# Splitting the p v products of an eight-key tile by keys instead of heads, with one VectorE sum, and moving GpSimd's residual add to the end of its slot

## The chip, the cores and the metric

One core of one Trainium2 chip runs the program once. The metric is the device time of that execution in microseconds (us).

## What is computed

The input x has shape 8 x 2048 x 512 (n, b, c). Attention runs over the first axis, so every (b, head) pair has a sequence of only 8 positions. The mask lets positions 0 to 3 see keys 0 to 3, and positions 4 to 7 see all eight.

```python
xn = layernorm(x)                                  # over c, eps 1e-5
q, k, v = split(xn @ Wqkv.T + bqkv)                # 16 heads of 32
scores = mask + 32**-0.5 * einsum('bnd,bmd->bnm', q, k)
attn = softmax(scores)
o = einsum('bnm,bmd->bnd', attn, v)
attn_out = o @ Wproj.T + bproj
lin = fp16(fp8(xn)) @ fp16(fp8(Wffn)).T + bffn     # float32 sums
out = x + attn_out + lin
```

## The kernel before

The 16,384 rows are cut into 128 tiles of 128 rows, so a tile is one position n % 8 for 128 values of b. Eight tiles in a row are a group, and their k and v stay in SBUF for the whole group (`k_all`, `v_all`, two groups deep; v is stored with the key as the innermost of its indices). The first four tiles of a group need 4 keys, the last four need 8.

The order is written out by hand. Each engine runs the same list of slots, and in slot j it does, for each stage, the tile j minus the stage's lag (`L_STATS` 1 to `L_PROJ` 15). Sixteen slots (two groups) are the body of a loop, `run_slots`; the first and the last sixteen stand outside it, and seven passes lie inside. Engines meet through counting semaphores alone (`after(...)`), and each works through its own queue strictly in the written order.

Slots are named here by j modulo 16. What bears on the change, per slot:

- **VectorE** (`slot` under `@block.vector`): layer-norm statistics (L722), the sum over keys of the p v products of tile j - 12 (L731), the aggregate of the statistics (L736), the q k products (L694) and their sum (L698) of tile j - 8, the softmax row sum and reciprocal of tile j - 9 (L745, L748), for an eight-key tile a second L694 and L698, then row maximum and shift (L758, L761). An eight-key tile takes two of the 2048-element products and sums, a four-key tile one. The lags make every slot hold three such units: slots 4 to 7 and 12 to 15 have two q k units and one p v sum, slots 0 to 3 and 8 to 11 have one q k unit and two p v sums.
- **GpSimd** (`slot` under `@block.gpsimd`): the probabilities (L399) and the first p v product of tile j - 11 (L388), the residual add of tile j - 15 (L407), the low half of the attention output of tile j - 13 (L412), the power for the inverse deviation of tile j - 2 (L418), the low half of the normalised x of tile j - 3 (L423), and for an eight-key tile the second p v product (L388 again). Slots 7 to 10 and 15, 0, 1, 2 have two products, the others one.
- **ScalarE**: exponential of tile j - 9 (L473), copies and scales for the layer norm (L482 to L510), high half of o (L491), the scaled copy `projected` (L516), the linear part and the preset of `proj_ps` (L522, L527), and the copies of k and v out of PSUM, tile j - 4 (L534, L543).
- **TensorE**: projection of tile j - 15, the linear product of tile j - 14, k and v of tile j - 4, q of tile j - 5.
- **SyncE's queue** issues, in this order: the load of x (L297), the reload for the residual (L301), the store of tile j - 15 (L306, after `y_ready`, the residual add's semaphore), the transpose of o (L316), that of x8 (L324) and that of x16 (L330).

The p v products go through a ring of four buffers of 2048 float32, `prod_pv`. For an eight-key tile, `head_units` gives two units of 8 heads and all 8 keys; for a four-key tile one unit of 16 heads and 4 keys:

```python
v = v_all[:, (n // N) % 2, h * D:(h + heads) * D, 0:keys].rearrange("p (h d) m -> p h d m", d=D)
p = probs[:, n % 2, h:h + heads, 0:keys].unsqueeze(2).broadcast_to([P, heads, D, keys])
```

## Time and profile before

| | |
|---|---|
| median of 3 runs | 1708.37 us (1707.04 to 1708.56) |
| the profiled execution's own time | 1709.81 us |
| its span, first to last instruction | 1707.7 us |
| mean granted TensorE clock in it | 0.978 |
| busy: TensorE, VectorE, GpSimd, ScalarE | 1517.0, 1518.7, 1373.5, 1025.5 us |

The profile is one execution. "Busy" is the time in which an engine executed something; an idle time is put down to the engine and line whose semaphore ended it, and "issue" is idle time for which the profile shows no such event. The span is the clock for all rows; 2.1 us of the execution lie around it.

### The profile page before, as it was taken

The numbers are of one execution on the slowest core, as the hardware profiler recorded it, in microseconds if no ns is written. First come the engines' busy times: TensorE is split into PE (matmuls) and PEld (weight loads), VectorE is DVE, ScalarE is ACT, GpSimd is POOL, SyncE is SP. The second block draws the span as 40 slices with busy tenths as digits, with TensorE's granted clock in tenths as the row PEclk, the third lists the DMA queues.
The fourth block names the chain that finished last, engine by engine and source line by source line (L and its number), as shares of the span: only waits on it lengthen the run. The fifth ranks groups of instructions, "written<-read, shape, count | busy, mean of one in ns | idle before, by whom it ended". The sixth has DMA issues, their size and how long they took to land.

```text
span 1707.7 us, 24850 instructions
## 1 busy us (share of the span) xinstructions
PE 1517.0 (89%) x6791; PEld 677.6 (40%) x6913; DVE 1518.7 (89%) x1380; ACT 1025.5 (60%) x1946; POOL 1373.5 (80%) x854
## 2 busy tenths in 40 slices
PE   4998898989989998998989899898998989899855
PEld 3443343434434443443434344343443434344312
DVE  6499898989989999999989899898998899999892
ACT  5665666656656666556566666666666666666422
POOL 2368879697896979879697887969788796978877
PEclk8999999999999999999999999999999999999978
DMA  5343534445354354444444444444444444453332
GB/s 188 72 99 90 123 99 109 117 99 130 98 124 105 97 130 98 117 112 111 109 105 113 106 116 105 114 111 101 119 105 119 105 105 116 104 124 85 90 71 77
DMA packets 366532, 184.30 MB, mean 108 GB/s; under 512 B 314160, under 2 KB 314160, under 8 KB 366384
## 3 DMA queue, kind: packets, MB, share of 16 engines
q1 hardware_dynamic: 366384, 182.53, 43.9%
q8 instruction: 68, 1.11, 0.3%
q14 instruction: 80, 0.66, 0.2%
HBM read 73.41 MB, written 33.55 MB: 63 GB/s over the span
## 4 chain that ended last, share of the span: by engine, by line
POOL 35%; issue 30%; DVE 26%; PE 4%; ACT 3%; POOLq 1%; DVEq 1%; DMA 0%; ACTq 0%; SPq 0%
POOL prod_pv L388 22%; DVE prod_qk L694 14%; DVE scores L698 6%; POOL o L412 4%; POOL x L423 4%; POOL xs L407 3%; POOL rstd L418 2%; DVE stats L722 2%; PE k_ps L579 1%; PE v_ps L579 1%; POOL probs L399 1%; DVE q_ps L758 1%; DVE row_sum L745 1%; PE q_ps L579 1%; POOLq L79 1%
## 5 line engine op out<-in xcount | busy, mean ns | idle before, releaser
L388 POOL TENSOR_TENSOR prod_pv<-kv,probs 128x2048 f32<-128x2048 f32 x192 | 813.0, 4234 | 16.2 <-POOL probs L399 11.1
L731 DVE TENSOR_REDUCE o_nat<-prod_pv 128x256 f32<-128x2048 f32 (+1 forms) x192 | 436.1, 2284 | 92.3 <-POOL prod_pv L388 72.5
L698 DVE TENSOR_REDUCE scores<-prod_qk 128x64 f32<-128x2048 f32 x192 | 439.4, 2288 | 7.3
L579 PE MATMUL k_ps<-wqkv_hi,xT 128*128 128x512 f16 x1024 | 334.1, 388 | 118.2 <-DMA xT<-x 118.1
L694 DVE TENSOR_TENSOR prod_qk<-q_ps,kv 128x2048 f32<-128x2048 f32 x192 | 432.0, 2250 | 2.5 <-ACT kv L534 2.5
L407 POOL TENSOR_TENSOR xs<-xs,projected 128x512 f32<-128x512 f32 x128 | 162.4, 1269 | 238.5 <-ACT projected L516 237.9
L579 PE MATMUL proj_ps<-wproj_hi,oT 128*128 128x512 f16 x1032 | 336.4, 388 | 6.3 <-ACT proj_ps L527 6.3
L579 PE MATMUL v_ps<-wqkv_hi,xT 128*128 128x512 f16 x1024 | 326.0, 380 | 0.0
L579 PE MATMUL q_ps<-wqkv_hi,xT 128*128 128x512 f16 x1024 | 325.4, 379 | 0.0
L473 ACT ACTIVATE exps<-shifted,exp_scale 128x64 f32<-128x64 f32 (+1 forms) x128 | 47.8, 373 | 365.8 <-DVE shifted L761 365.6
L579 PEld LDWEIGHTS k_ps<-wqkv_hi,xT 128*128 128x128 f16 x1024 | 101.8, 99 | 272.7 <-issue 144.8
L543 ACT ACTIVATE kv<-v_ps 128x512 f32<-128x512 f32 x128 | 141.3, 1104 | 113.9 <-PE v_ps L579 113.8
L579 PE MATMUL proj_ps<-wproj_lo,oT 128*128 128x512 f16 x516 | 201.1, 390 | 0.0
L579 PE MATMUL k_ps<-wqkv_lo,xT 128*128 128x512 f16 x512 | 198.9, 388 | 0.0
L579 PE MATMUL v_ps<-wqkv_lo,xT 128*128 128x512 f16 x512 | 194.5, 380 | 0.0
L579 PE MATMUL q_ps<-wqkv_lo,xT 128*128 128x512 f16 x512 | 194.0, 379 | 0.0
L423 POOL TENSOR_TENSOR x<-xn,x 128x512 f16<-128x512 f32 x128 | 148.3, 1159 | 17.4 <-ACT x L510 17.4
L534 ACT ACTIVATE kv<-k_ps 128x512 f32<-128x512 f32 x128 | 75.4, 589 | 133.1 <-PE k_ps L579 133.1
L412 POOL TENSOR_TENSOR o<-o_nat,o 128x512 f16<-128x512 f32 x128 | 148.3, 1159 | 5.6 <-ACT o L491 5.6
L579 PEld LDWEIGHTS proj_ps<-wproj_hi,oT 128*128 128x128 f16 x1032 | 102.7, 100 | 125.4 <-issue 9.8
L579 PEld LDWEIGHTS v_ps<-wqkv_hi,xT 128*128 128x128 f16 x1024 | 100.5, 98 | 121.8 <-issue 1.7
L579 PEld LDWEIGHTS q_ps<-wqkv_hi,xT 128*128 128x128 f16 x1024 | 100.2, 98 | 120.8
(115 smaller groups left out, 1727.9 us busy)
## 6 DMA issues: line engine op xcount, KB each, us to landing
xn<-in_L_attn_x SPq DMA_DIRECT2D x128, 256.0 KB, 2.8
xs<-in_L_attn_x SPq DMA_DIRECT2D x128, 256.0 KB, 2.9
out<-xs SPq DMA_DIRECT2D x128, 256.0 KB, 2.0
xT<-x SPq DMA_TRANSPOSE x256, 3.0
kv<-in_L_attn_Wqkv SPq DMA_DIRECT2D x3, 1024.0 KB, 10.6
oT<-o SPq DMA_TRANSPOSE x128, 3.2
kv<-in_L_ffn_weight SPq DMA_DIRECT2D x1, 1024.0 KB, 5.6
kv<-in_L_attn_Wproj SPq DMA_DIRECT2D x1, 1024.0 KB, 14.6
```

What stands on the lines that cost most here:

```text
L388: nc.gpsimd.tensor_tensor(o, v, p, ALU.mult).then_inc(pv_multiplied, 1)
L407: nc.gpsimd.tensor_tensor(xs[:, n % 4, :], xs[:, n % 4, :], projected[:, :], ALU.add).then_inc(y_ready, 1)
L412: nc.gpsimd.tensor_tensor(o16[:, n % 2, C:2 * C], o_nat[:, n % 2, :], o16[:, n % 2, 0:C], ALU.subtract).then_inc(o_lo_ready, 1)
L418: nc.gpsimd.tensor_tensor(rstd[:, n % 2, :], var_eps[:, :], minus_half[:, :], ALU.pow).then_inc(rstd_ready, 1)
L423: nc.gpsimd.tensor_tensor(x16[:, n % 2, C:2 * C], xn[:, n % 4, :], x16[:, n % 2, 0:C], ALU.subtract).then_inc(x_lo_ready, 1)
L473: nc.scalar.activation(exps[:, n % 4, :, 0:keys], shifted[:, :, 0:keys], ACT.Exp, scale=exp_scale[:, 0:1]).then_inc(exps_ready, 1)
L534: nc.scalar.activation(k_all[:, g % 2, n % N, :], k_ps[:, :], ACT.Copy).then_inc(k_kept, 1)
L543: nc.scalar.activation(v_all[:, g % 2, :, n % N], v_ps[:, :], ACT.Copy).then_inc(v_kept, 1)
L579: last = nc.tensor.matmul(acc[:, :], t[:, tc, :], w[:, c, col:col + 512], start=first and k == 0, stop=k == len(parts) - 1, skip_group_che ...
L694: nc.vector.tensor_tensor(prod_qk[:, :].rearrange("p (m c) -> p m c", c=C), qb, k, ALU.mult).then_inc(qk_multiplied, 1)
L698: nc.vector.tensor_reduce(scores[:, :, m0:m0 + 4].rearrange("p h m -> p m h"), prod_qk[:, :].rearrange("p (m h d) -> p m h d", h=H, d=D), ...
L731: nc.vector.tensor_reduce(o_nat[:, n % 2, h * D:(h + heads) * D], prod_pv[:, u % PRODS, :].rearrange("p (c m) -> p c m", m=keys), AX_X, AL ...
```

## The change

Two edits.

1. For an eight-key tile the two p v units are now keys 0 to 3 and keys 4 to 7 of all 16 heads (`key_units`, which the q k products use already); the function `head_units` is gone. Each unit's product has the shape that a four-key tile has: 16 heads, 32 channels, 4 keys. The two halves lie in neighbouring buffers of the ring, and VectorE sums both in one `tensor_reduce` over two axes (buffer and key), which waits for the tile's last product and raises `pv_summed` by two.
2. In GpSimd's slot the residual add stands last, behind the second product.

```diff
-            def products(i, n, unit):
-                u, h, heads = unit
-                keys = keys_of(n)
-                v = v_all[:, (n // N) % 2, h * D:(h + heads) * D, 0:keys].rearrange("p (h d) m -> p h d m", d=D)
-                p = probs[:, n % 2, h:h + heads, 0:keys].unsqueeze(2).broadcast_to([P, heads, D, keys])
-                o = prod_pv[:, u % PRODS, :].rearrange("p (h d m) -> p h d m", d=D, m=keys)
+            def products(i, n, u, m0):
+                v = v_all[:, (n // N) % 2, :, m0:m0 + 4].rearrange("p (h d) m -> p h d m", d=D)
+                p = probs[:, n % 2, :, m0:m0 + 4].unsqueeze(2).broadcast_to([P, H, D, 4])
+                o = prod_pv[:, u % PRODS, :].rearrange("p (h d m) -> p h d m", d=D, m=4)
                 after(pool, probs_ready, tile_count(i, n))
-                after(pool, v_kept, tile_count(i, N * (n // N) + keys - 1))
+                after(pool, v_kept, tile_count(i, N * (n // N) + m0 + 3))
                 after(pool, pv_summed, unit_count(i, u - PRODS))
                 nc.gpsimd.tensor_tensor(o, v, p, ALU.mult).then_inc(pv_multiplied, 1)
...
-                    products(i, n, head_units(n)[0])
-                if live(i, j, L_PROJ):
-                    n = j - L_PROJ
-                    after(pool, proj_scaled, tile_count(i, n))
-                    after(pool, res_loaded[n % 4], 16 * ring_count(i, n, 4))
-                    nc.gpsimd.tensor_tensor(xs[:, n % 4, :], xs[:, n % 4, :], projected[:, :],
-                                            ALU.add).then_inc(y_ready, 1)
+                    products(i, n, *key_units(n)[0])
...
-                    for unit in head_units(n)[1:]:
-                        products(i, n, unit)
+                    for unit in key_units(n)[1:]:
+                        products(i, n, *unit)
+                if live(i, j, L_PROJ):
+                    n = j - L_PROJ
+                    after(pool, proj_scaled, tile_count(i, n))
+                    after(pool, res_loaded[n % 4], 16 * ring_count(i, n, 4))
+                    nc.gpsimd.tensor_tensor(xs[:, n % 4, :], xs[:, n % 4, :], projected[:, :],
+                                            ALU.add).then_inc(y_ready, 1)
...
-                    keys = keys_of(n)
-                    for u, h, heads in head_units(n):
-                        after(dve, pv_multiplied, unit_count(i, u))
-                        after(dve, o_lo_ready, tile_count(i, n - 2))
-                        nc.vector.tensor_reduce(o_nat[:, n % 2, h * D:(h + heads) * D],
-                                                prod_pv[:, u % PRODS, :].rearrange("p (c m) -> p c m", m=keys), AX_X,
-                                                ALU.add).then_inc(pv_summed, 1)
+                    units = len(key_units(n))
+                    place = units_before(n) % PRODS
+                    after(dve, pv_multiplied, unit_count(i, last_unit(n)))
+                    after(dve, o_lo_ready, tile_count(i, n - 2))
+                    nc.vector.tensor_reduce(o_nat[:, n % 2, :],
+                                            prod_pv[:, place:place + units, :].rearrange("p q (c m) -> p c q m", m=4),
+                                            AX_XY, ALU.add).then_inc(pv_summed, units)
```

How the instructions stand. On GpSimd, slot 15 of the first pass, ahead of the jump back to the loop's start: L399 and L388 are the probabilities and a product, L407 the residual add, L412, L418 and L423 the low half of o, the power and the low half of x. Before:

```order
L399 TENSOR_TENSOR probs<-exps,inv_sum 128x128 [waits pv_multiplied,inv_ready]
L388 TENSOR_TENSOR prod_pv<-kv,probs 128x2048 [waits pv_summed,v_kept,probs_ready]
L407 TENSOR_TENSOR xs<-xs,projected 128x512 [waits res_loaded0,proj_scaled]
L412 TENSOR_TENSOR o<-o_nat,o 128x512 [waits o_hi_ready]
L418 TENSOR_TENSOR rstd<-var_eps,minus_half 128x1 [waits xn_ready,var_ready]
L423 TENSOR_TENSOR x<-xn,x 128x512 [waits x_hi_q_ready]
L388 TENSOR_TENSOR prod_pv<-kv,probs 128x2048 [waits pv_summed,v_kept,probs_ready]
L93 UNCONDITIONAL_BRANCH
```

and with the change (the lines of the changed program are numbered anew):

```order
L392 TENSOR_TENSOR probs<-exps,inv_sum 128x128 [waits pv_multiplied,inv_ready]
L381 TENSOR_TENSOR prod_pv<-kv,probs 128x2048 [waits pv_summed,v_kept,probs_ready]
L399 TENSOR_TENSOR o<-o_nat,o 128x512 [waits o_hi_ready]
L405 TENSOR_TENSOR rstd<-var_eps,minus_half 128x1 [waits xn_ready,var_ready]
L410 TENSOR_TENSOR x<-xn,x 128x512 [waits x_hi_q_ready]
L381 TENSOR_TENSOR prod_pv<-kv,probs 128x2048 [waits pv_summed,v_kept,probs_ready]
L420 TENSOR_TENSOR xs<-xs,projected 128x512 [waits res_loaded0,proj_scaled]
L88 UNCONDITIONAL_BRANCH
```

The add has gone from the third place to the last, and the jump now follows it instead of a product.

On VectorE, slot 0 of the loop, where an eight-key tile is summed. Before:

```order
L722 BN_STATS stats<-xn 128x6 [waits mean_var_ready]
L79 REGISTER_ALU
L79 ISA [waits stats_ready,minus_mean_ready]
L79 REGISTER_ALU [waits pv_multiplied]
L731 TENSOR_REDUCE o_nat<-prod_pv 128x256 [waits o_lo_ready]
L79 REGISTER_ALU
L731 TENSOR_REDUCE o_nat<-prod_pv 128x256 [waits o_lo_ready,pv_multiplied]
L736 BN_AGGR mean_var<-stats 128x2
```

and with the change:

```order
L715 BN_STATS stats<-xn 128x6 [waits mean_var_ready]
L74 REGISTER_ALU
L74 ISA [waits stats_ready,minus_mean_ready]
L74 REGISTER_ALU [waits pv_multiplied]
L724 TENSOR_REDUCE o_nat<-prod_pv 128x512 [waits o_lo_ready]
L729 BN_AGGR mean_var<-stats 128x2
```

Two sums, each with its own wait for a product, have become one that waits for both products.

SyncE's queue, one slot of the loop, with the change (the same as before but for the line numbers):

```order
L292 DMA xn<-in_L_attn_x 128x512
L296 ISA [waits y_stored2]
L296 DMA xs<-in_L_attn_x 128x512
L301 ISA [waits y_ready]
L301 DMA out<-xs 128x512
L74 REGISTER_ALU
L311 DMA_TRANSPOSE oT<-o 128x8x128 [waits o_lo_ready,proj_summed]
L319 DMA_TRANSPOSE xT<-x 128x2x128 [waits x_hi_q_ready,lin_summed]
L74 REGISTER_ALU [waits x_lo_ready]
L325 DMA_TRANSPOSE xT<-x 128x8x128 [waits q_summed]
```

Nothing moved here: the store, with its wait for the residual add, still stands ahead of the three transposes.

## Rows read from the trace of the kernel before

**Rows 1.** Windows, one pass: length, busy PE, PEld, DVE, ACT, POOL, clock

```profile
755.70:957.50 201.80, 184.47 (x837) 82.36 (x851) 186.29 (x168) 126.15 (x242) 170.71 (x105) 1.00 0.46 110
```

**Rows 2.** Groups by line, shapes apart, VectorE: passes of the loop, then tail

```profile
L731 DVE TENSOR_REDUCE o_nat<-prod_pv 128x256 f32<-128x2048 f32 x112 | 253.5, 2284 | 66.6 <-POOL prod_pv L388 59.3 <-DVE stats L722 6.0
...
L731 DVE TENSOR_REDUCE o_nat<-prod_pv 128x256 f32<-128x2048 f32 x10 | 22.6, 2281 | 7.6 <-POOL prod_pv L388 7.6
...
L731 DVE TENSOR_REDUCE o_nat<-prod_pv 128x256 f32<-128x2048 f32 x7 | 15.9, 2277 | 15.8 <-POOL o L412 10.1 <-POOL prod_pv L388 5.7
```

**Rows 3.** Timeline of VectorE (start us, duration us, what, idle before it)

```profile
853.31 0.69 DVE L722 BATCH_NORM_STATS2 stats<-xn 128x6 f32<-128x512 f32 x1
854.03 4.48 DVE L731 TENSOR_REDUCE o_nat<-prod_pv 128x256 f32<-128x2048 f32 x2
858.43 0.17 DVE L736 BATCH_NORM_AGGREGATE mean_var<-stats 128x2 f32<-128x6 f32 x1
...
863.88 0.69 DVE L722 BATCH_NORM_STATS2 stats<-xn 128x6 f32<-128x512 f32 x1
...
893.97 2.29 DVE L731 TENSOR_REDUCE o_nat<-prod_pv 128x256 f32<-128x2048 f32 x1 [2.96 <-POOL prod_pv L388]
...
914.55 0.69 DVE L722 BATCH_NORM_STATS2 stats<-xn 128x6 f32<-128x512 f32 x1
...
927.66 0.69 DVE L722 BATCH_NORM_STATS2 stats<-xn 128x6 f32<-128x512 f32 x1
...
957.55 0.69 DVE L722 BATCH_NORM_STATS2 stats<-xn 128x6 f32<-128x512 f32 x1 [3.58 <-issue]
```

**Rows 4.** Timeline of GpSimd: starts of slots 9 and 10, then slot 15 into slot 0

```profile
866.85 0.42 POOL L399 TENSOR_TENSOR probs<-exps,inv_sum 128x128 f32<-128x128 f32 x1
...
880.38 0.42 POOL L399 TENSOR_TENSOR probs<-exps,inv_sum 128x128 f32<-128x128 f32 x1
...
945.52 1.27 POOL L407 TENSOR_TENSOR xs<-xs,projected 128x512 f32<-128x512 f32 x1 [4.21 <-ACT projected L516]
...
948.38 1.16 POOL L423 TENSOR_TENSOR x<-xn,x 128x512 f16<-128x512 f32 x1
949.50 4.53 POOL L388 TENSOR_TENSOR prod_pv<-kv,probs 128x2048 f32<-128x2048 f32 x1
953.99 0.40 POOL L399 TENSOR_TENSOR probs<-exps,inv_sum 128x128 f32<-128x128 f32 x1
```

**Rows 5.** GpSimd's products by tile: duration ns, shortest, median, longest

```profile
L388 POOL TENSOR_TENSOR prod_pv<-kv,probs x192: 3637/4523/4558, 91.5 to 1683.6; 128x2048 f32<-128x2048 f32 x192
```

**Rows 6.** Groups by line, shapes apart, VectorE: row sum with 8 and 4 keys

```profile
L745 DVE TENSOR_REDUCE row_sum<-exps 128x16 f32<-128x128 f32 x64 | 17.6, 276 | 0.0
...
L745 DVE TENSOR_REDUCE row_sum<-exps 128x16 f32<-128x64 f32 x64 | 13.4, 209 | 2.8 <-ACT exps L473 2.8
```

**Rows 7.** Timeline of ScalarE: copy of v in slot 10, start of slot 13

```profile
885.93 1.11 ACT L543 ACTIVATE kv<-v_ps 128x512 f32<-128x512 f32 x1 [1.36 <-PE v_ps L579]
...
914.67 0.40 ACT L473 ACTIVATE exps<-shifted,exp_scale 128x128 f32<-128x128 f32 x1 [1.11 <-DVE shifted L761]
...
917.96 0.61 ACT L510 ACTIVATE x<-xn 128x512 fp8e4<-128x512 f32 x1
918.48 0.66 ACT L516 ACTIVATE projected<-proj_ps,out_scale 128x512 f32<-128x512 f32 x1
```

**Rows 8.** Timeline of TensorE: first product of k in slots 10 and 12

```profile
880.54 0.39 PE L579 MATMUL k_ps<-wqkv_hi,xT 128*128 128x512 f16 x1 [1.94 <-DMA xT<-x]
...
907.06 0.39 PE L579 MATMUL k_ps<-wqkv_hi,xT 128*128 128x512 f16 x1 [1.33 <-DMA xT<-x]
```

**Rows 9.** SyncE: a wait in total, times, longest us; two issues of slot 11

```profile
SPq L306 <- POOL xs L407: 763.0, 128, 10.9
...
902.02 1.17 SPq L324 DMA_TRANSPOSE xT<-x  x1
903.37 1.23 SPq L330 DMA_TRANSPOSE xT<-x  x1
```

4 lines of the change are left out of this document (1 added, 3 removed).

## The prediction

> **What bounds the kernel now.** I read the busy time of one pass of the loop first. Of its 201.8 us VectorE works 186.3, TensorE 184.5 and GpSimd 170.7 [rows 1]. No average names a bound there, so a slot-by-slot reading is needed. The lags of the slots decide the rest.
>
> For VectorE I take a slot from one statistics instruction to the next. Without a stall, a slot with two q k units takes 927.66 - 914.55 = 13.11 us, and one with two p v sums takes 863.88 - 853.31 = 10.57 [rows 3]. GpSimd's slots with two products take 880.38 - 866.85 = 13.53 us without a gap in them [rows 4]. These are slots 7 to 10 and 15 to 2, and three of each four fall on VectorE's short slots. There VectorE stands still until the second product is done, 2.96 us at a time [rows 3]. Grouped by line, the two sums of eight-key tiles waited 59.3 us for products inside the passes, 7.6 us in the slots right behind the passes, and 15.8 us in the tail [rows 2].
>
> So two engines take turns: GpSimd in its heavy slots, VectorE in the rest. GpSimd cannot work ahead for its heavy stretch: in slot 15 it sits idle for 4.21 us because the residual add, third in its slot, needs `projected`, which ScalarE delivers late in its own slot [rows 4]. One more stall is in every pass: 3.58 us ahead of VectorE's first instruction after the jump back, ended by nothing the profile shows [rows 3]. Nothing in the change touches it.
>
> **Part 1, the shape of the products.** GpSimd's 192 products have the same number of elements, yet two durations: 3.64 us at the short end, 4.52 in the middle [rows 5]. The 64 short ones are the four-key tiles' (16 heads, 32 channels, 4 keys), the 128 long ones the eight-key tiles' (8 heads, 8 keys; 4.53 us in slot 15 [rows 4]). The change gives those 128 the short form. The first unit reads by the very pattern of a four-key tile. The second starts at the fifth key, 16 bytes further, which no row shows: its price lies between 3.64 and 4.53 us. I take 3.64, because the form is the same and only the start differs. Then a heavy slot takes 13.53 - 2 x 0.89 = 11.75 us.
>
> The Trainium skill speaks against this: its "GPSIMD Engine Reference", section "Performance versus the Vector engine", gives a two-input elementwise instruction a floor of about 2.5 cycles per element, and 4497 ns for 2048 float32, whatever the pattern. That agrees with the eight-key products and not with the four-key ones, which are 0.86 us shorter; if it held for the new ones, nothing would be gained in this part (rival 2 works that case out from rows).
>
> **Part 2, one sum for two.** Two sums occupy VectorE for 858.43 - 854.03 = 4.40 us, 2.20 each [rows 3]. The row sum costs 276 ns for 128 elements and 209 for 64 [rows 6], so 1.05 ns per element; 2048 of them are 2.14 us and the fixed part is 0.06. One instruction for 4096 elements saves that once: 64 x 0.06 = 3.8 us. It reads 16-byte pieces from two places 8 KB apart in turn. The nearest row, the 64-element row sum, also takes 16-byte pieces (at a step of 32) and pays nothing per element for it. Bounds: 4.33 us as reckoned; an upper one no row gives (rival 3).
>
> The new wait is the larger matter: the sum cannot start on the first half. Queued behind it on VectorE are the aggregate and the next q k product. It must not come before GpSimd's second product is done, which Part 4 checks.
>
> **Part 3, the add at the end.** Let S be the start of VectorE's slot. ScalarE starts at S + 0.12; the low half of x can start when x8 is done, at S + 4.0, and `projected` is done at S + 4.6 [rows 7]. With the add last, GpSimd no longer waits for `projected` ahead of 4.5 us of product, but for x8, ahead of 1.1 + 3.6.
>
> What the add is moved past: the low halves of o and x, the second product, and, through `y_ready`, SyncE's queue. There the store stands ahead of the three transposes, and already waits 763.0 us in total for the add [rows 9]. Call E the end of the add. In a heavy slot E comes one product and one add after the low half of x, and only then the transposes are issued: about 0.5 us for the store (an estimate from its short issue), 1.5 for the transpose of o (estimated by the next one), 903.37 - 902.02 = 1.35 for that of x8, and 3.7 from the last one's issue to TensorE's first k product (903.37 to 907.06 [rows 8, 9]), so **k starts at E + 7.1**. The copy of v follows 885.93 - 880.54 = 5.4 us later and takes 1.1 [rows 7, 8], and ScalarE's next slot starts behind it, at E + 13.6. That is two slots after the one of E.
>
> The jump follows the add (1.27 us) instead of a product (4.53), which hid GpSimd's own refetch, since its next instruction starts without a gap [rows 4]. If it costs what VectorE's does, 3.58 + 0.29 - 1.27 = 2.6 us are uncovered. VectorE stands still there too, so I count nothing.
>
> **Part 4, does GpSimd keep up?** Slot 7: low half of x at S + 4.0 to 5.2, second product to 8.8, E at 10.0. Slot 8 (S is 13.1 later): probabilities and first product end at S + 1.0, the rest waits for x8 again: E = S + 10.0. Slot 9 (10.6 later): first product to S + 3.5, three small steps to 6.3, second product to 9.9, E = 11.1. Slot 10: second product ends at S + 11.0. VectorE wants it for the sum of slot 11 at S(11) + 0.7, which is S(10) + 11.3. So it is in time by 0.3 us, and all earlier ones by more. The way through the transposes: E of slot 8 is S(10) - 11.2, so ScalarE starts slot 10 at S + 2.4 instead of 0.1, x8 is done at 6.3, and the second product ends at 11.1: in time by 0.2. TensorE idles some 2 us in slots 8 and 9, and makes it up in 12 to 15, where its 184.5 / 16 = 11.5 us per slot stand against 13.1.
>
> After the jump VectorE's stall gives 3.5 us more room. **So every slot is VectorE's**, with two places where a few tenths decide.
>
> **The sum.** From 1707.7: products' waits in the passes 59.3, after them 7.6 [rows 2], the merged sums 3.8. The tail is GpSimd's. Its heavy slots lack the power and the low half of x there (1.16 us, and some 0.5 of the 3.98 from the add's start to the second product's [rows 4]), so they take 11.8 us and will take 10.0: three of them give 5.4. The last sum costs 2.1 more, since both halves follow the last product. An estimated 0.5 comes back where a wait for `projected` no longer precedes a product. That is 3.8. Together 74.5, a span of 1633.2, with the 2.1 around it 1635.3. The median stands 1.4 below the profiled execution: **1634 us**.
>
> **Rivals.**
>
> 1. *The queue behind the store costs more.* The slack of 0.2 us is gone if the transposes land, say, 2 us later (three are now issued in one burst), or if only the second product keeps 4.53. Then slots 10 and 11 stall 2 us, twice a pass less what the jump hides, say 20 us in seven passes and 2 behind them: **1656 us**. For it: the small slack, and that all 128 stores come first. Against: even tied to this path throughout, two heavy slots would take 13.6 + 9.8 = 23.4 us against 27.0 now, so it cannot undo the gain.
> 2. *The form brings nothing:* products of 4.53 us from a cause other than the form. Heavy slots stay at 13.5; the second product of slot 8 ends at S + 9.7, that of slot 9 13.5 later, at S(9) + 12.6, where the sum of slot 10 wants it at S(9) + 11.3 (a stall of 1.3), and that of slot 10 another 13.5 later, 2.9 after the sum of slot 11 is due. Behind the jump the same reckoning, with 2.6 us uncovered there, gives 0.7 and 2.9. That is 7.8 a pass against 59.3 / 7 = 8.5 now, and with the merged sums a gain of 10: **1698 us**. Against: the four-key rows have no other difference than form.
> 3. *Slower: the two-axis sum pays for its jumps.* The gain is 74 us over 64 sums, so it decides from 1.2 us more per sum, 5.5 instead of 4.3. At twice the time per element (8.6 us) 64 sums add 64 x 4.3 = 275 us in slots that VectorE bounds: **1909 us**. For it: no row shows such a read. Against: the row sums. The Trainium skill's "SBUF — State Buffer", section "Door 1: The DMA port swizzle", has full bandwidth for accesses that stay in a 16-byte line, which each piece of four float32 does; no run here shows it for this pattern.
>
> **How the numbers follow.** Forecast 0.74, rival 1 0.12, rival 2 0.07, rival 3 0.05, something else near no change 0.02. The range holds the forecast and rival 1. Below it reaches to 1616: the 6.0 us of waits between statistics and sum [rows 2] could go as well, and the 5.7 us of product waits in the tail. Above it reaches to 1684, for a rival 1 of twice the size. A measurement can tell 0.2%, 3.4 us, from no change. Faster: 0.92 (forecast, rivals 1 and 2, less 0.01); same 0.02; slower 0.06.
>
> **What would show it.** Right: all 192 products near 3.64 us; 64 sums near 4.35 us; VectorE's idle time before p v sums in the passes below 10 us; a pass of about 193 us; k starting late after its transpose in slots 8 to 11; GpSimd's waits no longer ahead of the add but ahead of the low halves. Wrong: products of two durations in one tile, sums above 5 us, or VectorE waiting for q, k or the exponential, which would mean that the path through the transposes binds.

## The result, and the profile after

The changed kernel takes **1623.88 us** (median of 4 runs, 1623.51 to 1624.54) where the kernel before takes 1708.46 beside it (4 runs, 1707.04 to 1709.53): a ratio of 0.9506, with an interval of 0.9489 to 0.9522. It is faster by 84.6 us. The forecast was 1634 with a range of 1616 to 1684, so the direction and the range were right, and the point lies 10 us above the time. That small miss is the sum of larger ones with opposite signs, and most of what follows is about them.

The profiled execution took 1623.51 us, its span 1621.7. First the page of the changed kernel: the busy time of each engine, and one of the queues.

```profile
PE 1503.6 (93%) x6791; PEld 677.0 (42%) x6913; DVE 1512.6 (93%) x1316; ACT 1032.9 (64%) x1946; POOL 1265.4 (78%) x854
...
q14 instruction: 50, 0.41, 0.1%
```

GpSimd is busy for 1265.4 us where it was 1373.5. The second line is a queue that fetches instructions, in packets of 8 KB (0.41 MB / 50). There were 80 packets before and there are 50 now, five fewer for each of the loop's six jumps.

The window of the same pass of the loop answers to [rows 1], with the same columns:

```profile
718.95:909.18 190.23, 183.66 (x834) 82.25 (x849) 185.56 (x161) 127.02 (x241) 156.78 (x105) 1.00 0.48 117
```

A pass takes 190.23 us instead of 201.80. VectorE works 185.56 of them, so this pass is VectorE's but for 4.7 us, as Part 4 had it. GpSimd has 33 us to spare.

GpSimd's products, by tile (count; shortest, median, longest in ns), answer to [rows 5]:

```profile
L381 POOL TENSOR_TENSOR prod_pv<-kv,probs x192: 3634/3642/3656, 91.1 to 1592.3; 128x2048 f32<-128x2048 f32 x192
```

All 192 have one duration. VectorE's groups by line with the shapes apart answer to [rows 2]. The first three rows are of the whole span, the fourth of the passes alone, the fifth of the stretch from the last statistics instruction to the end.

```profile
L724 DVE TENSOR_REDUCE o_nat<-prod_pv 128x512 f32<-128x4096 f32 x64 | 282.9, 4420 | 24.7 <-POOL prod_pv L381 16.7 <-DVE stats L715 3.6 <-ACT minus_mean L477 1.8
...
L715 DVE BATCH_NORM_STATS2 stats<-xn 128x6 f32<-128x512 f32 x128 | 88.2, 689 | 14.4 <-DMA xn<-in_L_attn_x 11.9 <-issue 2.2
```
```profile
L724 DVE TENSOR_REDUCE o_nat<-prod_pv 128x512 f32<-128x4096 f32 x56 | 247.5, 4420 | 10.7 <-DVE stats L715 3.4 <-POOL prod_pv L381 3.0 <-ACT minus_mean L477 1.8
...
L724 DVE TENSOR_REDUCE o_nat<-prod_pv 128x512 f32<-128x4096 f32 x8 | 35.4, 4419 | 14.1 <-POOL prod_pv L381 13.7 <-DVE stats L715 0.2 <-issue 0.2
```

In the passes the sums wait 3.0 us for products, where they waited 59.3 [rows 2]. The stall ahead of the first statistics instruction after the jump, 20.5 us over six jumps before (of which [rows 3] show one of 3.58), is down to 2.2. Nothing in the forecast had that.

VectorE's timeline in the slots that answer to [rows 3]: the sum of slot 8, that of slot 11, which still waits, and the jump.

```profile
814.98 4.42 DVE L724 TENSOR_REDUCE o_nat<-prod_pv 128x512 f32<-128x4096 f32 x1
...
845.68 0.69 DVE L715 BATCH_NORM_STATS2 stats<-xn 128x6 f32<-128x512 f32 x1
846.73 4.42 DVE L724 TENSOR_REDUCE o_nat<-prod_pv 128x512 f32<-128x4096 f32 x1 [0.37 <-POOL prod_pv L381]
...
909.18 0.69 DVE L715 BATCH_NORM_STATS2 stats<-xn 128x6 f32<-128x512 f32 x1 [0.31 <-issue]
```

The sum of slot 11 waits 0.37 us, once a pass. The forecast had it in time by 0.3 (by 0.2 on the other way). GpSimd's timeline answers to [rows 4]: slot 15 before, a heavy slot, then the jump.

```profile
802.92 1.16 POOL L399 TENSOR_TENSOR o<-o_nat,o 128x512 f16<-128x512 f32 x1 [4.25 <-ACT o L484]
...
805.18 1.16 POOL L410 TENSOR_TENSOR x<-xn,x 128x512 f16<-128x512 f32 x1 [0.59 <-ACT x L503]
...
824.24 0.41 POOL L392 TENSOR_TENSOR probs<-exps,inv_sum 128x128 f32<-128x128 f32 x1
...
835.98 0.41 POOL L392 TENSOR_TENSOR probs<-exps,inv_sum 128x128 f32<-128x128 f32 x1
...
904.48 1.27 POOL L420 TENSOR_TENSOR xs<-xs,projected 128x512 f32<-128x512 f32 x1
905.71 0.41 POOL L392 TENSOR_TENSOR probs<-exps,inv_sum 128x128 f32<-128x128 f32 x1
```

A heavy slot takes 835.98 - 824.24 = 11.74 us (13.53 before; 11.75 forecast). GpSimd's idle time now stands ahead of the low halves. Across the jump it has no gap, though only the short add precedes it: the 2.6 us of a possible gap, which the forecast took to be covered by VectorE's stall, do not occur at all. The waits over the span say the same (us, times, longest):

```profile
POOL o L399 <- ACT o L484: 199.0, 79, 5.8
...
POOL x L410 <- ACT x L503: 60.3, 83, 1.8
PE k_ps L572 <- DMA xT<-x: 47.6, 38, 6.8
...
POOL xs L420 <- ACT projected L509: 24.2, 42, 4.1
```

The wait for `projected` was 237.9 us and is 24.2. TensorE's for the transposes of x is less than half of the 118.1 it was.

**Where 86.0 us of the span went.** The first stretch ends at the first statistics instruction of the loop, the second at the last one of all (1559.50 before, 1479.52 after), the third at the tail's first heavy sum (1656.10 and 1570.28), the fourth at the end.

| stretch | before | after | gained | forecast |
|---|---|---|---|---|
| before the loop | 148.2 | 147.9 | 0.3 | 0 |
| passes | 1411.3 | 1331.6 | 79.7 | 59.3 + 3.4 = 62.7 |
| slots behind them | 96.6 | 90.8 | 5.8 | 7.6 + 0.2 = 7.8 |
| tail | 51.6 | 51.4 | 0.2 | 3.8 + 0.2 = 4.0 |

In the passes 56 us are the idle time ahead of the sums (66.6 to 10.7), 18.3 the stall at the jump, 3.4 the merged sums, and 2 are spread.

### The profile page after: what moved, and what is told of

Its sections match the earlier page's. It is cut to its first block, busy times and chain, and to the rows that moved or that the text cites. A ratio compares the mean times of both kernels' runs of the same rounds, so it can differ in the third digit from the quotient of the medians.

```text
span 1621.7 us, 24736 instructions
## 1 busy us (share of the span) xinstructions
PE 1503.6 (93%) x6791; PEld 677.0 (42%) x6913; DVE 1512.6 (93%) x1316; ACT 1032.9 (64%) x1946; POOL 1265.4 (78%) x854
## 4 chain that ended last, share of the span: by engine, by line
POOL 43%; issue 29%; DVE 10%; PE 7%; ACT 1%; POOLq 1%; DMA 0%; SPq 0%; DVEq 0%; ACTq 0%
POOL prod_pv L381 28%; DVE prod_qk L687 5%; POOL xs L420 5%; POOL x L410 4%; POOL o L399 3%; DVE scores L691 2%; POOL rstd L405 2%; POOL probs L392 2%; PE k_ps L572 2%; PE v_ps L572 2%; PE proj_ps L572 1%; PE q_ps L572 1%; DVE stats L715 1%; POOLq L74 1%; PE lin_ps L610 0%
## 5 line engine op out<-in xcount | busy, mean ns | idle before, releaser
L381 POOL TENSOR_TENSOR prod_pv<-kv,probs 128x2048 f32<-128x2048 f32 x192 | 699.4, 3642 | 16.2 <-POOL probs L392 11.1
L724 DVE TENSOR_REDUCE o_nat<-prod_pv 128x512 f32<-128x2048 f32 (+1 forms) x128 | 429.1, 3353 | 27.0 <-POOL prod_pv L381 16.7
L572 PE MATMUL k_ps<-wqkv_hi,xT 128*128 128x512 f16 x1024 | 328.0, 381 | 49.4 <-DMA xT<-x 47.6
L399 POOL TENSOR_TENSOR o<-o_nat,o 128x512 f16<-128x512 f32 x128 | 148.6, 1161 | 199.0 <-ACT o L484 199.0
L420 POOL TENSOR_TENSOR xs<-xs,projected 128x512 f32<-128x512 f32 x128 | 162.5, 1270 | 24.7 <-ACT projected L509 24.2
L509 ACT ACTIVATE projected<-proj_ps,out_scale 128x512 f32<-128x512 f32 x128 | 87.4, 683 | 86.0 <-PE proj_ps L572 74.3
## 6 DMA issues: line engine op xcount, KB each, us to landing
kv<-in_L_attn_Wproj SPq DMA_DIRECT2D x1, 1024.0 KB, 14.7
```

What stands on the lines that cost most here:

```text
L381: nc.gpsimd.tensor_tensor(o, v, p, ALU.mult).then_inc(pv_multiplied, 1)
L399: nc.gpsimd.tensor_tensor(o16[:, n % 2, C:2 * C], o_nat[:, n % 2, :], o16[:, n % 2, 0:C], ALU.subtract).then_inc(o_lo_ready, 1)
L420: nc.gpsimd.tensor_tensor(xs[:, n % 4, :], xs[:, n % 4, :], projected[:, :], ALU.add).then_inc(y_ready, 1)
L509: nc.scalar.activation(projected[:, :], proj_ps[:, :], ACT.Copy, scale=out_scale[:, 0:1]).then_inc(proj_scaled, 1)
L572: last = nc.tensor.matmul(acc[:, :], t[:, tc, :], w[:, c, col:col + 512], start=first and k == 0, stop=k == len(parts) - 1, skip_group_che ...
L724: nc.vector.tensor_reduce(o_nat[:, n % 2, :], prod_pv[:, place:place + units, :].rearrange("p q (c m) -> p c q m", m=4), AX_XY, ALU.add).t ...
```

## The experiments

### The two edits apart

`e1_add_last_alone` moves the add and leaves products and sums as they were.

```diff
                     products(i, n, head_units(n)[0])
-                if live(i, j, L_PROJ):
-                    n = j - L_PROJ
...
                         products(i, n, unit)
+                if live(i, j, L_PROJ):
+                    n = j - L_PROJ
...
+                    nc.gpsimd.tensor_tensor(xs[:, n % 4, :], xs[:, n % 4, :], projected[:, :],
+                                            ALU.add).then_inc(y_ready, 1)
```

> The kernel before with the second edit alone: the residual add at the end of GpSimd's slot, products still by heads and two sums. Theory (the shape of the products carries the gain, the add's place only lets GpSimd begin its heavy stretch earlier): products stay at 4.53 us, heavy slots at 13.5 us; VectorE's waits for products in the passes stay near 50 to 60 us, the stall behind the jump stays near 3.5 us; 1690 to 1705 us. Rival (the place of the add carries the gain): waits for products mostly gone, below 1660 us.

Measured: 1689.85 us (1689.26 to 1690.5), ratio 0.9885 (0.9868 to 0.9901), 20.7 us faster. Its VectorE groups:

```profile
L731 DVE TENSOR_REDUCE o_nat<-prod_pv 128x256 f32<-128x2048 f32 x128 | 287.9, 2281 | 37.1 <-POOL prod_pv L388 20.1 <-POOL o L406 9.9 <-DVE stats L722 6.0
...
L722 DVE BATCH_NORM_STATS2 stats<-xn 128x6 f32<-128x512 f32 x128 | 88.3, 690 | 60.0 <-DMA xn<-in_L_attn_x 36.2 <-issue 23.3
```

The waits for products fall from 72.5 to 20.1, but 24 of these 52 us turn into a new wait of the statistics for their rows of x (36.2 against 11.9). The loads of x are issued by SyncE behind the store and the transposes. With products of 4.53 us the add is late, and all that stands behind the store in that queue is late with it; that this is what delays the rows is read from the order of the queue and not tested by a run.

`e2_split_alone` makes the other half of the change, products by four keys and the merged sum, and leaves the add where it was.

```diff
-                    products(i, n, head_units(n)[0])
+                    products(i, n, *key_units(n)[0])
                 if live(i, j, L_PROJ):
...
-                    for u, h, heads in head_units(n):
-                        after(dve, pv_multiplied, unit_count(i, u))
...
+                    after(dve, pv_multiplied, unit_count(i, last_unit(n)))
...
+                                            prod_pv[:, place:place + units, :].rearrange("p q (c m) -> p c q m", m=4),
+                                            AX_XY, ALU.add).then_inc(pv_summed, units)
```

> The changed kernel with the residual add back in the third place. Theory (both edits are needed): the add waits for `projected` at S + 4.6 in slots 7 and 15, and each heavy slot's second product ends at about S + 12.2, so the sums of slots 9, 10, 11 and 1, 2, 3 wait 1.0 to 1.3 us each, some 6.8 us a pass: 1665 to 1675 us. Rival (the shorter products alone are enough): within 5 us of the changed kernel's 1623.9.

Measured: 1665.69 us (1665.21 to 1666.22), ratio 0.9743 (0.9727 to 0.976).

```profile
L724 DVE TENSOR_REDUCE o_nat<-prod_pv 128x512 f32<-128x4096 f32 x64 | 282.9, 4420 | 72.4 <-POOL prod_pv L381 69.0 <-ACT minus_mean L477 2.1 <-DVE stats L715 0.5
```

The shorter products alone save hardly any waiting (69.0 us for products, against 72.5): the merged sum waits for both products, 1.2 to 1.4 us in five slots of a pass and 0.4 in a sixth, since GpSimd now spends its shorter product waiting for `projected` (307.8 us in total, against 237.9). Of the 44.9 us gained, 18 are the stall at the jump, which is gone here too (the idle time ahead of the statistics falls from 32.7 to 14.8 us), 18 the idle time ahead of the sums (90.0 to 72.4 over the span), and 4 the merged sums. The edits need each other: alone they save 20.7 and 44.9 us, together 84.6, which is 19 more than the sum.

### The merged sum, and the stall at the jump

`e3_two_sums` keeps the change but splits the merged sum into two instructions of half the channels, both behind both products.

```diff
+                    for q in range(units):
+                        c0, c1 = q * C // units, (q + 1) * C // units
...
-                                            prod_pv[:, place:place + units, :].rearrange("p q (c m) -> p c q m", m=4),
+                                                prod_pv[:, place:place + units, 4 * c0:4 * c1].rearrange(
+                                                    "p q (c m) -> p c q m", m=4),
```

> The changed kernel, but an eight-key tile is summed by two instructions again, each over half the channels and both key buffers, behind the same wait for both products. VectorE's loop has 231 instructions instead of 223 (235 before the change). Theory A (the stall behind the jump, 3.58 us before and 0.32 after, hangs on the length or place of VectorE's code): it comes back to about 3 us in six passes, and the sums cost 0.07 us more each: 1640 to 1648 us. Theory B (the stall went because VectorE no longer reaches the jump late or early, that is by timing, not by code): it stays near 0.3 us, 1628 us.

Measured: 1647.9 us (1645.4 to 1650.22), ratio 0.9634 (0.9617 to 0.965), 24 us slower than the change.

```profile
L726 DVE TENSOR_REDUCE o_nat<-prod_pv 128x256 f32<-128x2048 f32 x128 | 286.7, 2281 | 21.1 <-POOL prod_pv L381 15.4 <-DVE stats L715 4.7
...
L715 DVE BATCH_NORM_STATS2 stats<-xn 128x6 f32<-128x512 f32 x128 | 88.2, 689 | 39.1 <-issue 26.2 <-DMA xn<-in_L_attn_x 12.6
```

The products' waits are nearly the same. The difference is the stall: 26.2 us, 4.4 per jump. So the stall is tied to the program of VectorE, not to what GpSimd does. The loop has eight instructions more than the change's, or ten if the waits for semaphores are counted too (more on that count below). Length, or place? Two kernels ask that with the same twelve tiny memsets of about 0.06 us each, once in the loop and once ahead of it.

`e5_loop_padded`:

```diff
                     n = j - L_STATS
+                    if j < 12:
+                        nc.vector.memset(filler[:, j:j + 1], 0.0)
```

> The changed kernel with a one-element VectorE memset in slots 1 to 11 of every 16 and in slot 0 once a pass: 12 more instructions, so VectorE's loop has 235, as before the change, and starts 11 instructions later in its program. Theory (the stall behind the jump hangs on VectorE's code): it comes back to 3 to 4.5 us in six passes; with about 0.1 us for each memset 1650 to 1660 us. Rival (timing, not code): the stall stays near 0.3 us, about 1632 us.

`e5p_before_loop`:

```diff
             low_parts(0, KC)
+            for f in range(12):
+                nc.vector.memset(filler[:, f:f + 1], 0.0)
```

> The changed kernel with the same 12 memsets in VectorE's setup instead: the loop keeps its 223 instructions but ends where the loop of the kernel before ended (instruction 360 of its program). If the length of the loop decides, the stall stays near 0.3 us and the time within 3 us of 1623.9. If the place of its end decides, the stall comes back to 3 to 4.5 us: 1643 to 1650 us. The memsets themselves cost about 1 us, once.

Measured: 1645.93 us (1644.03 to 1646.59, ratio 0.9628, 0.9612 to 0.9644) with the memsets in the loop, and 1645.5 (1645.08 to 1646.16, ratio 0.9627, 0.9611 to 0.9643) with them ahead of it. The second in its passes:

```profile
L718 DVE BATCH_NORM_STATS2 stats<-xn 128x6 f32<-128x512 f32 x113 | 77.7, 688 | 24.2 <-issue 24.2
```

Twelve instructions that run once, outside the loop, cost 21.6 us. The loop's own code is untouched. It is the loop's **place** in VectorE's program that decides. Two further kernels move it further, with the same diff and another count.

`e12_loop_one_block_on`: the changed kernel with 132 memsets ahead of the loop, which shifts e5p's loop by 120 instructions.

> The changed kernel with 132 one-element memsets in VectorE's setup, so that its loop of 223 instructions stands 132 places later (257 to 480) instead of 12 (137 to 360, which brought the stall back). If code is brought in by blocks and what counts is how the loop lies on them, a shift by about one block (an estimate from instruction packets of about 8 KB and 64 bytes per instruction: 128) leads back to the case of no shift, and the stall is again near 0.3 us: 1624 us and some 8 us for the memsets. If any loop that ends behind instruction 350 stalls, it is 3 us or more: 1650 us or more.

`e13_before_shifted`: the kernel before with 112 such memsets.

> The kernel before with 112 one-element memsets in VectorE's setup, so that its loop of 235 instructions stands at 237 to 472 instead of 125 to 360. The loops seen without a stall behind the jump (125 to 348, 257 to 480) would lie on two blocks of 128 if a border were between 348 and 352, those with a stall (125 to 356, 125 to 360, 137 to 360, 136 to 371) on three. By that this loop lies on two, and the stall goes to 0.3 us. Theory (before the change GpSimd's heavy slots bound the slots behind the jump, so the stall was covered): VectorE's waits for products grow by what the stall loses, and the time stays within 4 us of the kernel before. Rival (the stall cost its full length before as well): 16 to 20 us faster.

Measured: 1626.66 us (one run) for the changed kernel with 132. The stall is gone again, and so are the packets that came with it:

```profile
q14 instruction: 51, 0.42, 0.1%
```
```profile
L718 DVE BATCH_NORM_STATS2 stats<-xn 128x6 f32<-128x512 f32 x128 | 88.1, 688 | 14.2 <-DMA xn<-in_L_attn_x 11.9 <-issue 2.0
```

It is 2.8 us above the change, less than what the memsets delay the loop's start by (152.77 us against 147.93). For the kernel before with 112, 1726.29 us (1725.44 to 1727.09), ratio 1.0105 (1.0088 to 1.0121): **17.6 us slower**, where I had expected either no difference or one of that size the other way. Its queue q14 has 81 packets. VectorE's statistics, over the span and at one jump:

```profile
L725 DVE BATCH_NORM_STATS2 stats<-xn 128x6 f32<-128x512 f32 x128 | 88.1, 688 | 47.6 <-issue 35.2 <-DMA xn<-in_L_attn_x 12.2
```
```profile
969.78 0.69 DVE L725 BATCH_NORM_STATS2 stats<-xn 128x6 f32<-128x512 f32 x1 [5.36 <-issue]
```

The stall did not go, it grew, from 20.5 to 35.2 us. That is 14.7 of the 17.6; another 3.0 is the longer start (first statistics instruction of the loop at 151.18 instead of 148.21).

Here is where each loop lies in VectorE's program, and what a jump cost. The second column counts instructions without the waits for semaphores, as the expectations above do. But the built program holds most waits as instructions of their own, and the third column counts those too. The traces bear the third column out: between two of VectorE's jumps they record 379 instructions in the kernel before and 365 with the change, not 235 and 223.

| kernel | loop from, to | with the waits | stall per jump, us |
|---|---|---|---|
| before | 125, 360 | 220, 599 | 3.4 |
| the change | 125, 348 | 220, 585 | 0.3 |
| two sums | 125, 356 | 220, 595 | 4.4 |
| 12 memsets in the loop | 136, 371 | 231, 608 | 4.0 |
| 12 ahead of it | 137, 360 | 232, 597 | 4.0 |
| 132 ahead of it | 257, 480 | 352, 717 | 0.3 |
| before, 112 ahead | 237, 472 | 332, 711 | 5.8 |

What the runs show is that a jump costs 0.3 or 3.4 to 5.8 us, that a shift of 12 brings the stall, and that a further one of 120 takes it away. The expectation of `e13_before_shifted` rested on blocks of 128 in the second column, with a border between 348 and 352. That run speaks against it: its loop lay on two such blocks and stalled the most.

By the third column all seven rows fit a simple picture: the program is fetched in blocks of 256 instructions, one border lies between 589 and 595, and a jump is free where the loop touches two blocks (220 to 585, 352 to 717) and stalls where it touches three (all others; 332 to 711 begins just ahead of the border one block below). The rows do not tell this from blocks of 128 of which three are held. Either picture was made to fit the rows and was not tested by a run of its own. In the first picture the 132 memsets shift the loop by half a block, not by one. So it is in part luck that the expectation of `e12_loop_one_block_on` came true. Why the last row costs more than the rest stays open, and the place is not all: `e1_add_last_alone` has the very VectorE program of the kernel before and pays 3.9 us per jump instead of 3.4. The Trainium skill, "Runtime: NRT & Kernel Launch", section "Instruction fetch mechanics", has an engine hold two blocks of its program, of 256 instructions each, and a taken branch outside them stall. The stalls agree with that, with the waits counted.

### The order in GpSimd's and SyncE's slots

`e7_add_before_second` puts the add between the low half of x and the second product.

```diff
-                if live(i, j, L_PV):
-                    n = j - L_PV
-                    for unit in key_units(n)[1:]:
-                        products(i, n, *unit)
                 if live(i, j, L_PROJ):
...
+                if live(i, j, L_PV):
+                    n = j - L_PV
+                    for unit in key_units(n)[1:]:
+                        products(i, n, *unit)
```

> The changed kernel with the residual add between the low half of x and the second product. SyncE's store and transposes leave some 3.6 us earlier in a heavy slot, but the second product ends 1.25 us later. Theory (the slack of GpSimd's second product before the sums of slots 3 and 11 is the tight place): those sums wait 1 to 1.5 us more each, 1632 to 1642 us. Rival (the late transposes are the tight place): 1618 to 1624 us.

Measured: 1632.89 us (1632.4 to 1634.02), ratio 0.9555 (0.9539 to 0.9571), 9 us slower than the change.

```profile
L724 DVE TENSOR_REDUCE o_nat<-prod_pv 128x512 f32<-128x4096 f32 x64 | 282.9, 4420 | 38.2 <-POOL prod_pv L381 31.0 <-DVE stats L715 3.6 <-ACT minus_mean L477 2.1
```

The waits for products nearly double, 16.7 to 31.0 us. So the second product is the tight place of the slot, as the small slack in Part 4 had it, and not the way through store and transposes, which this order relieves.

`e6_store_last` leaves GpSimd alone and puts SyncE's store behind its three transposes.

```diff
-                if live(i, j, L_PROJ):
-                    n = j - L_PROJ
-                    after(sp, y_ready, tile_count(i, n))
-                    sp.dma_start(out_v[n % N, i + n // PAIR, (n // N) % 2],
-                                 xs[:, n % 4, :]).then_inc(y_stored[n % 4], 16)
...
                     sp.dma_start_transpose(xT[:, n % XT, :, :], x16[:, n % 2, :]).then_inc(xT_moved[n % XT], 16)
+                if live(i, j, L_PROJ):
+                    n = j - L_PROJ
+                    after(sp, y_ready, tile_count(i, n))
+                    sp.dma_start(out_v[n % N, i + n // PAIR, (n // N) % 2],
+                                 xs[:, n % 4, :]).then_inc(y_stored[n % 4], 16)
```

> The changed kernel, but SyncE's queue issues the store, with its wait for the residual add, behind the slot's three transposes instead of ahead of them. Theory (VectorE bounds every slot; the late transposes are covered): TensorE's waits for transposes fall (47.6 us on k after the change), VectorE's slots keep their length: within 4 us of 1623.9. Rival (the path store, transposes, k, v, ScalarE still costs VectorE time): 6 to 15 us faster.

Measured: 1621.14 us (1620.91 to 1621.57), ratio 0.9483 (0.9467 to 0.9498), 2.7 us faster than the change. TensorE's waits for the transposes of x go from 47.6 to 17.6 us and ScalarE waits 477.6 us for VectorE instead of 98.6, so everything upstream runs earlier. Yet the passes take 1331.5 us against 1331.6: VectorE sets them, and the path through the transposes has slack. The gain of 2.5 us in the span is all in the tail, where the changed kernel shows this (SyncE's issues; GpSimd's low half of o and add; TensorE's start of the next projection; VectorE's last sum; last add of all):

```profile
1591.17 1.15 POOL L399 TENSOR_TENSOR o<-o_nat,o 128x512 f16<-128x512 f32 x1
...
1595.88 1.26 POOL L420 TENSOR_TENSOR xs<-xs,projected 128x512 f32<-128x512 f32 x1
...
1596.02 4.42 DVE L724 TENSOR_REDUCE o_nat<-prod_pv 128x512 f32<-128x4096 f32 x1 [5.59 <-POOL prod_pv L381]
...
1597.17 0.34 SPq L301 DMA_DIRECT2D out<-xs  x1
...
1597.70 1.29 SPq L311 DMA_TRANSPOSE oT<-o  x1
...
1601.30 0.61 PE L601 MATMUL proj_ps<-out_bias_rows,ones 128*128 128x512 bf16 x1 [4.35 <-DMA oT<-o]
...
1617.90 1.26 POOL L420 TENSOR_TENSOR xs<-xs,projected 128x512 f32<-128x512 f32 x1 [4.07 <-ACT projected L509]
```

and the kernel before this:

```profile
1682.52 1.15 POOL L412 TENSOR_TENSOR o<-o_nat,o 128x512 f16<-128x512 f32 x1
...
1683.83 1.25 SPq L316 DMA_TRANSPOSE oT<-o  x1
...
1686.99 0.61 PE L608 MATMUL proj_ps<-out_bias_rows,ones 128*128 128x512 bf16 x1 [6.33 <-DMA oT<-o]
1688.09 1.26 POOL L407 TENSOR_TENSOR xs<-xs,projected 128x512 f32<-128x512 f32 x1
1688.17 2.29 DVE L731 TENSOR_REDUCE o_nat<-prod_pv 128x256 f32<-128x2048 f32 x1 [2.11 <-POOL prod_pv L388]
...
1703.93 1.26 POOL L407 TENSOR_TENSOR xs<-xs,projected 128x512 f32<-128x512 f32 x1 [4.07 <-ACT projected L516]
```

Before, the transpose of o was issued 0.16 us behind the low half of o (1683.67 to 1683.83). After, the store ahead of it in the queue waits for an add that itself stands behind a product of 3.64 us, and the transpose goes out 5.4 us behind it (1592.32 to 1597.70). Three residual adds, 5.3 us apart, still have to follow (1607.28, 1612.57 and 1617.90). So the time from the end of the last sum to the end of the program grew from 17.2 us (1690.46 to 1707.7) to 21.3 (1600.44 to 1621.7). With the store last it is 18.7, its last sum ending at 1600.52 and its span at 1619.2, and the transpose goes out as soon as its data is there:

```profile
1591.26 1.15 POOL L399 TENSOR_TENSOR o<-o_nat,o 128x512 f16<-128x512 f32 x1
```
```profile
1592.57 1.25 SPq L306 DMA_TRANSPOSE oT<-o  x1
```

So the queue explains 2.6 of the 4.1 us. The other 1.5 stay with the moved add itself. In this kernel the next projection waits no longer for the transpose but for ScalarE's preset of `proj_ps`, which stands behind `projected`, and that waits until the late add has read the `projected` before:

```profile
1597.32 0.69 ACT L509 ACTIVATE projected<-proj_ps,out_scale 128x512 f32<-128x512 f32 x1 [6.15 <-POOL xs L420]
```
```profile
1599.32 0.38 PE L601 MATMUL proj_ps<-out_bias_rows,ones 128*128 128x512 bf16 x1 [4.29 <-ACT proj_ps L520]
```

### What makes a product short

The forecast took the form (16 heads by 4 keys) for the cause of 3.64 us. Two kernels keep that form and change only which keys a unit reads. `e8_interleaved_keys` takes the even keys and then the odd ones, in v and in p alike, so that each group of four is spread over 32 bytes instead of 16.

```diff
+                keys = slice(0, 4) if n % N < PROMPT else slice(m0 // 4, m0 // 4 + 7, 2)
-                v = v_all[:, (n // N) % 2, :, m0:m0 + 4].rearrange("p (h d) m -> p h d m", d=D)
-                p = probs[:, n % 2, :, m0:m0 + 4].unsqueeze(2).broadcast_to([P, H, D, 4])
+                v = v_all[:, (n // N) % 2, :, keys].rearrange("p (h d) m -> p h d m", d=D)
+                p = probs[:, n % 2, :, keys].unsqueeze(2).broadcast_to([P, H, D, 4])
...
-                after(pool, v_kept, tile_count(i, N * (n // N) + m0 + 3))
+                after(pool, v_kept, tile_count(i, N * (n // N) + (3 if n % N < PROMPT else 7)))
```

> The changed kernel with the halves of an eight-key tile taken as even and odd keys: still 16 heads and 4 keys a product, but v and p are read at a step of 8 bytes, so that each group of four comes from two 16-byte pieces. If the count of keys in the innermost dimension sets the products' time, they stay at 3.64 us and the time within 4 us of 1623.9. If it is how the reads fall on 16-byte pieces, the 128 products slow down to 4.5 us or more and the time to 1670 us or more.

`e9_p_from_two_pieces` does it for p alone. It leaves v contiguous and so multiplies values by the probabilities of other keys.

```diff
+                keys = slice(0, 4) if n % N < PROMPT else slice(m0 // 4, m0 // 4 + 7, 2)
-                p = probs[:, n % 2, :, m0:m0 + 4].unsqueeze(2).broadcast_to([P, H, D, 4])
+                p = probs[:, n % 2, :, keys].unsqueeze(2).broadcast_to([P, H, D, 4])
```

> The changed kernel with v read as in the change (four neighbouring keys) but the probabilities of an eight-key tile taken as even and odd keys, so that only p comes from two 16-byte pieces; the pairing of p with v, and so the result of those tiles, is changed by it. Reading both at a step of two keys cost 5.45 us a product. If the repeated operand p makes the difference between one piece (3.64) and two (4.53, by heads), the 128 products cost about 4.5 us here. If it is v, they stay at 3.64.

Measured: 1803.21 us (1800.35 to 1803.91), ratio 1.0546 (1.0528 to 1.0563), for the first, and 1705.31 (one run) for the second. Their products by tile:

```profile
L382 POOL TENSOR_TENSOR prod_pv<-kv,probs x192: 3637/5451/5502, 92.5 to 1770.0; 128x2048 f32<-128x2048 f32 x192
```
```profile
L382 POOL TENSOR_TENSOR prod_pv<-kv,probs x192: 3638/4602/4634, 91.1 to 1672.9; 128x2048 f32<-128x2048 f32 x192
```

The form is the same in all three, the durations are 3.64, 4.60 and 5.45 us. So it is not the number of heads and keys that counts. What fits is how many 16-byte pieces each operand's group takes: one each 3.64, two for p 4.60, two for both 5.45. The two kernels also read at a step of 8 bytes instead of 4, and no run parts that from the pieces; the units by heads, which have no such step and pay too, speak for the pieces. The units by heads of the kernel before took groups of eight keys, two pieces each read in order, at 4.53 [rows 5]. That p has the larger part in it (0.96 of 1.81 us) is from these two kernels. That the old units paid for p alone, since v is read once in order, is only argued.

### The best version

`e10_store_last_tail_on_vector` is `e6_store_last` with the second product of the last three tiles moved to VectorE, which sits idle there.

```diff
+def on_vector(i, n):
+    return isinstance(i, int) and i * PAIR + n >= TILES - 3
...
-                        products(i, n, *unit)
+                        if not on_vector(i, n):
+                            products(i, n, *unit)
...
+                    if on_vector(i, n):
...
+                        nc.vector.tensor_tensor(
+                            prod_pv[:, u % PRODS, :].rearrange("p (h d m) -> p h d m", d=D, m=4),
+                            v_all[:, (n // N) % 2, :, m0:m0 + 4].rearrange("p (h d) m -> p h d m", d=D),
+                            probs[:, n % 2, :, m0:m0 + 4].unsqueeze(2).broadcast_to([P, H, D, 4]),
+                            ALU.mult).then_inc(tail_multiplied, 1)
```

> The changed kernel with the store last in SyncE's queue (1621.1 us by itself) and, for the last three tiles, the second product on VectorE (2.25 us in the place of 3.64 on GpSimd), where it waits 5.6 us a slot for GpSimd. Theory: the tail's slots of 10.0 us become 10.0 - 3.6 = 6.4 or VectorE's 2.25 + 4.4 = 6.7 us: three times 3.3 us, 1611 us. Rival: the tail then hangs on the low half of o, its transpose and the projection as well, and gains 3 us at most: 1618 us.

Measured: 1620.03 us (5 runs, 1619.33 to 1620.95), ratio 0.9482 (0.9468 to 0.9495). It is the lowest median of the study, 3.9 us below the change, but only 1.1 below `e6_store_last`. Their ranges overlap and their ratios to the kernel before are the same (0.9482 and 0.9483), so the runs do not tell the two apart. Two of the tail's slots shrank as the theory had it: from sum to sum they take 6.70 and 6.77 us instead of 10.02 and 10.01. But the one before them grew from 5.70 to 10.47. The timelines of VectorE and GpSimd show why:

```profile
1575.70 5.56 DVE L738 TENSOR_TENSOR prod_pv<-kv,probs 128x2048 f32<-128x2048 f32 x1
...
1585.69 2.28 DVE L738 TENSOR_TENSOR prod_pv<-kv,probs 128x2048 f32<-128x2048 f32 x1
```
```profile
1575.48 3.64 POOL L386 TENSOR_TENSOR prod_pv<-kv,probs 128x2048 f32<-128x2048 f32 x1 [0.99 <-DVE o_nat L748]
1579.08 3.20 POOL L408 TENSOR_TENSOR o<-o_nat,o 128x512 f16<-128x512 f32 x1
...
1585.94 5.53 POOL L386 TENSOR_TENSOR prod_pv<-kv,probs 128x2048 f32<-128x2048 f32 x1 [2.08 <-DVE o_nat L748]
```

The two engines do not run such products at full speed side by side. VectorE's product starts 0.22 us behind GpSimd's and lasts 5.56 us, and GpSimd's keeps its 3.64. Ten microseconds later VectorE's is first and keeps 2.28, and GpSimd's lasts 5.53. Each time the later one pays about what was left of the earlier one (3.42 and 2.03 us), and GpSimd's low half of o, caught behind VectorE's product, lasts 3.20 instead of 1.16. The Trainium skill, "GPSIMD Engine Reference", section "Specifications", has the two engines share their SBUF interfaces, with contention where VectorE's instruction has two SBUF inputs. These rows agree. In the loop VectorE's own product, which reads q from PSUM, keeps its 2.25 us and GpSimd's its 3.64; that this is because of PSUM is not tested by a run.

## Why the prediction was right, and where not

**What bounds the kernel.** Two engines taking turns, GpSimd by its heavy slots and by the late add: right. Each edit alone left waits in place, and over the span they show it: for products 72.5 us before, 20.1 with the add alone (and 24 more for rows of x), 69.0 with the products alone, 16.7 with both. In the passes both together took them from 59.3 to 3.0.

**Part 1.** Products of 3.64 us, heavy slots of 11.75: measured 3.64 and 11.74. The reason given, "the form is the same and only the start differs", is too weak. The form was the same in the two kernels on keys and gave 4.60 and 5.45. What the two units share is that each group lies in one 16-byte piece, and the old units by heads differed from the four-key tiles in that as well, though rival 2 was argued against with "no other difference than form". The floor that the forecast set against this part, 4497 ns, does not hold here, for any of the 192. The Trainium skill's "GPSIMD Engine Reference", section "Performance versus the Vector engine", gives that time for an add with about 2.6 cycles per element and names no pattern; "whatever the pattern" was the forecast's own addition. Rival 2 falls.

**Part 2.** A sum of 4.33 us: the instruction lasts 4.42 and the next one starts 4.34 behind its start (1570.28 to 1574.62), so 0.06 saved per sum as reckoned. It pays nothing for its jumps of 8 KB, which ends rival 3. Its wait for both products costs 0.37 us in one slot of a pass.

**Part 3.** GpSimd's waits moved from the add to the low halves, as forecast. Of the jump it said of VectorE's 3.58 us: "Nothing in the change touches it". **This is the step that failed.** The merged sum takes 14 instructions from VectorE's loop (12 without the waits for semaphores), and with them the stall, 18.3 us in all. A row of before showed the stall, and the forecast treated what "nothing the profile shows" ended as a constant of the jump, although the change altered the very code that is jumped over. With the stall put back by a shift of 12 instructions the changed kernel takes 1645.5 us. That is 11.5 us above the point of 1634, and the time that came is 10.1 below it. The point missed by about as much either way, so its nearness says little for the sum, and the range would have held either time.

**Part 4.** Every slot VectorE's: right. Slack of 0.3 and 0.2 us at slot 11: measured a wait of 0.37, so the reckoning was off by some 0.6 us, and 3.0 us in the passes came of it. From the end of slot 8 to that product GpSimd stands idle for 0.16 us at most at a time, so it is its own way that binds. TensorE was to start k late in slots 8 to 11 and to idle some 2 us in slots 8 and 9. It did, by a little less, and waited 0.16 us in slot 11:

```profile
817.85 0.39 PE L572 MATMUL k_ps<-wqkv_hi,xT 128*128 128x512 f16 x1 [1.59 <-DMA xT<-x]
...
830.98 0.39 PE L572 MATMUL k_ps<-wqkv_hi,xT 128*128 128x512 f16 x1 [1.52 <-DMA xT<-x]
```

From the end of slot 8's add (824.28) to k it is 6.7 us where 7.1 was reckoned, so the way through the transposes is a little shorter, and with the store last its waits fell by 30 us with no effect on a pass. Rival 1 did not occur, for want of that path's weight.

**The sum.** Against the kernel with the stall kept, the passes gained 1411.3 - 1352.9 = 58.4 us (its first statistics instruction of the loop at 148.91, the last at 1501.82), where 62.7 was forecast; its stalls of 24.2 instead of 20.5 and its 2.6 us of products' waits explain that, less the 2 that are spread. Behind the passes 7.8 was forecast and 5.8 came, because two sums still wait 1.46 and 0.24 us. In the tail the slots of 10.0 us came as forecast (1586.00 to 1596.02), and from its first sum to the end of its last 34.4 us became 30.2. But of the rest, "An estimated 0.5 comes back where a wait for `projected` no longer precedes a product" had the wrong sign: 4.1 us were lost there, 2.6 to the transpose of o behind the store behind the moved add, and 1.5 to `projected`, which is not free until the moved add has read it. Part 3 had named exactly this queue, for the loop, and it was not asked in the tail, where no slack hides it. In all the span gained 86.0 us where 74.5 was forecast: 18.3 for the stall were missing from the sum, and some 7 in it did not come (1.3 in the passes, 2.0 in the slots behind them, 3.8 in the tail). The median stands 1.4 us nearer to the forecast, because that had taken it 1.4 below the profiled execution and it is 0.4 above.

**The chances.** Faster at 0.92 was well founded, since every rival but one was faster too. The ends of the range do not follow from what is named for them. The 6.0 and 5.7 us of waits take 1634 to 1622.3 and not to 1616, and a rival 1 of twice the size gives 1634 + 2 x 22 = 1678 and not 1684. The stall that went was in neither.

## What to carry to other kernels

A stall behind a loop's jump that nothing in the profile ends can belong to the code's place and length: expect that it may change, by 3 to 6 us per jump here, with any edit that adds or takes instructions in or ahead of the loop, and compare two versions only after looking at that row and at the count of instruction packets. Where an instruction is moved to the end of an engine's slot, go through the queue behind its signal, and what its input's buffer holds up, once more for the tail, where the neighbours that covered it are gone. Judge a rearranged access by how each group of its operands lies in memory, here by its 16-byte pieces, and not by the count of its elements.
